# The ninth product of a tile's first quarter goes to SBUF and its transfer folds four planes

## What is computed

```python
x = x + _L0_conv_ref(_gn(x), ...)   # signs, 3x3 depthwise, prelu, bn, sign, 1x1, prelu, bn, + residual
x = x + _L1_conv_ref(_gn(x), L1_conv_W, L1_conv_b)

def _L1_conv_ref(x, W, b):          # K = 3
    filters = einsum('bchw,oc->bohw', x, W) + b            # 9 filters for each channel and pixel
    filters = filters.reshape(B, C, 9, H, Wd).transpose(0, 1, 3, 4, 2)
    patches = _extract_patches(x)                          # the 9 neighbours of each pixel
    return sum(patches * filters, axis=-1)
```

## Time and profile before

| what | us |
|---|---|
| median of three runs | 720.24 |
| the profiled execution | 720.51 |
| span of that execution | 718.6 |
| DVE busy | 657.9 |
| PE busy | 623.5 |
| POOL busy | 603.3 |
| ACT busy | 553.6 |
| DMA, queue of the folds (q0), share of 16 engines | 58.3% |
| DMA, queue of loads, stores and mirrors (q1), share | 27.8% |

### The profile page before, as it was taken

How to read it: one execution, slowest core, us unless ns; L and a number is a source line. 1 busy time by engine, 2 the same in 40 slices (tenths; PEclk the granted TensorE clock), 3 DMA queues, 4 the chain that set the end, 5 groups by cost and what they waited for, 6 DMA issues and landing times.

```text
span 718.6 us, 18827 instructions
## 1 busy us (share of the span) xinstructions
PE 623.5 (87%) x8017; PEld 254.4 (35%) x8017; DVE 657.9 (92%) x998; ACT 553.6 (77%) x822; POOL 603.3 (84%) x264
## 2 busy tenths in 40 slices
PE   2539889899998989899898989899999989899897
PEld 1224333333333334343333334333333334342333
DVE  3729879999999999999999999999999999999886
ACT  6885998897979788887978898897979888836110
POOL 2002658899999999989899999999999999999896
PEclk9859989999999999999999999999999999999899
DMA  5225767899999999998999999999999997998884
GB/s 202 87 58 148 131 153 196 190 251 207 227 226 196 233 203 245 205 252 187 230 219 182 244 204 250 206 246 215 223 229 193 240 202 162 203 191 176 193 172 136
DMA packets 34280, 142.11 MB, mean 198 GB/s; under 512 B 3348, under 2 KB 11540, under 8 KB 32276
## 3 DMA queue, kind: packets, MB, share of 16 engines
q0 software_dynamic: 17232, 75.87, 58.3%
q1 hardware_dynamic: 16940, 65.03, 27.8%
q10 hardware_dynamic: 24, 0.00, 0.0%
HBM read 26.03 MB, written 25.69 MB: 72 GB/s over the span
## 4 chain that ended last, share of the span: by engine, by line
POOL 48%; DVE 30%; ACT 7%; issue 6%; PE 4%; DMA 3%; SPq 1%; POOLq 0%; DVEq 0%; ACTq 0%
DVE prod L946 25%; POOL prod L386 17%; POOL ob L410 10%; POOL prod L399 10%; POOL prod L368 6%; POOL prod L377 3%; DVE xb L917 3%; PE tap_ps L478 3%; DMA mirror<-q 2%; ACT unused L581 2%; POOL prod L392 2%; ACT st L581 1%; ACT signs L581 1%; ACT ab L581 1%; DMA xb<-in_x_dram 1%
## 5 line engine op out<-in xcount | busy, mean ns | idle before, releaser
L478 PE MATMUL tap_ps<-q,w_t 64*64 64x392 f32 x2304 | 472.1, 506 | 52.1 <-DMA mirror<-q 20.5
L946 DVE SCALAR_TENSOR_TENSOR prod<-tap_ps,bias,q 128x784 f32<-128x784 f32 x493 | 487.4, 1026 | 31.4 <-PE tap_ps L478 26.0
L478 PE MATMUL tap_ps<-mirror,w_t 64*64 64x392 f32 x2304 | 467.4, 507 | 0.0
L478 PEld LDWEIGHTS tap_ps<-q,w_t 64*64 64x64 f32 x2304 | 151.2, 134 | 263.1 <-DVE prod L946 172.6
L386 POOL TENSOR_TENSOR prod<-prod 128x2352 f32<-128x2352 f32 x45 | 240.2, 5337 | 0.0
L368 POOL DMA_DIRECT2D prod<-prod x63 | 75.0, 1190 | 91.3 <-DVE prod L946 91.0
L521 PE MATMUL tap_ps<-signs,dw_diag 64*64 64x392 bf16 x2304 | 135.5, 342 | 9.8 <-DVE dw_diag L846 1.8
L478 PEld LDWEIGHTS tap_ps<-mirror,w_t 64*64 64x64 f32 x2304 | 139.4, 134 | 0.4 <-issue 0.4
L581 ACT ACTIVATE ab<-tap_ps,col 128x784 bf16<-128x784 f32 x128 | 120.5, 993 | 18.1 <-PE tap_ps L521 18.0
L410 POOL TENSOR_TENSOR ob<-prod 128x784 f32<-128x784 f32 x63 | 124.8, 1981 | 6.8 <-POOL prod L399 0.5
L581 ACT ACTIVATE st<-st 128x1 f32<-128x1 f32 x368 | 88.6, 252 | 36.5 <-DVE st L794 24.7
(11 more groups left out here) (117 smaller groups left out, 309.5 us busy)
## 6 DMA issues: line engine op xcount, KB each, us to landing
prod<-prod POOLq DMA_DIRECT2D x63, 1176.0 KB, 10.1
out_dram<-ob SPq DMA_DIRECT2D x31, 784.0 KB, 7.4
xb<-in_x_dram SPq DMA_DIRECT2D x15, 1568.0 KB, 15.7
mirror<-q SPq DMA_DIRECT2D x64, 203.0 KB, 4.3
xb<-in_x_dram SPq DMA_DIRECT2D x2, 784.0 KB, 5.8
out_dram<-ob SPq DMA_DIRECT2D x2, 392.0 KB, 2.3
prod<-in_L_conv_W_dram SPq DMA_DIRECT2D x1, 288.0 KB
prod<-in_L_conv_pw_weight_dram SPq DMA_DIRECT2D x1, 32.0 KB
```

Source lines behind the costliest of these rows:

```text
L478: mm = pe.matmul(rows3(tap_ps[to, slot, side, 0:CH]), w_t[own, k, :], moving, start=True, stop=True)
L946: v.scalar_tensor_tensor(place.rearrange("p j (a b) -> p j a b", b=WD), psum.rearrange("p j (a b) -> p j a b", b=WD), s_(t, B4) if k == 4 ...
```

## The change

In quarter 0 of all tiles but the last the ninth product now goes to SBUF like that of the other quarters (`POOLED` has 0 too), so that DVE's pair and POOL's early sum fall away there and ACT adds the mean to plane 8. Its fold (`fold_four`) waits for eight products and adds planes 0 to 3 onto planes 4 to 7. POOL's wide sum adds planes 6 and 7 onto 4 and 5, `add35` adds plane 8 onto 4, and the output sum takes planes 5 and 4. `PAIRED` is empty, so the branches of `in_pairs` make nothing. The delays of the steps on a quarter change, and with them most offsets in `COURSE`, `EARLY` and `PROLOGUE`, by 0 to 13 units.

```diff
+        def in_fours(g):
+            return on_pool(g) and g % QUARTERS in FOURS
...
+            def fold_four(t, qq):
+                g = quarter(t, qq)
+                wait(pool, prod_done, KK * g + 8)
+                pool.dma_start(prod[:, g % BUFS, 4:8, :], prod[:, g % BUFS, 0:4, :], accum_op=ALU.add,
+                               max_dma_last_dim=8 * QP).then_inc(folded[g % BUFS], 16)
...
                 pool.wait_ge(folded[g % BUFS], 16 * (g // BUFS + 1))
-                if on_pool(g):
+                if in_fours(g):
+                    pool.tensor_tensor(pr[:, 4:6, :], pr[:, 4:6, :], pr[:, 6:8, :], ALU.add).then_inc(summed_wide, 1)
+                elif on_pool(g) and not in_pairs(g):
                     pool.wait_ge(mean_added, with_mean(g))
...
-                if on_pool(g):
+                if in_fours(g):
+                    pool.wait_ge(summed_wide, g + 1)
+                    pool.wait_ge(mean_added, with_mean(g))
+                    pool.tensor_tensor(pr[4], pr[4], pr[8], ALU.add).then_inc(summed35, 1)
...
-                pool.tensor_tensor(ob[:, qq, :], pr[3], pr[4], ALU.add).then_inc(summed, 1)
+                pool.tensor_tensor(ob[:, qq, :], pr[5] if in_fours(g) else pr[3], pr[4], ALU.add).then_inc(summed, 1)
             for g in units:
-                for what, delay in ((fold, FOLD_DELAY), (add_early, EARLY_ADD_DELAY), (add_wide, WIDE_ADD_DELAY),
+                for t, qq in quarters(g, FOLD_DELAY):
+                    if not in_fours(quarter(t, qq)) and not (t.last and qq == QUARTERS - 1):
+                        fold(t, qq)
+                for t, qq in quarters(g, FOLD_FOUR_DELAY):
+                    if in_fours(quarter(t, qq)):
+                        fold_four(t, qq)
+                for what, delay in ((add_early, EARLY_ADD_DELAY), (add_wide, WIDE_ADD_DELAY),
                                     (add35, LATE_ADD_DELAY), (final, OUT_DELAY)):
...
 COURSE = {
-    'load': -106,
+    'load': -104,
...
-    'var1': -11,
-    'root1': -10,
-    'invert1': -10,
-    'q0': -8,
+    'var1': -12,
+    'root1': -11,
+    'invert1': -11,
+    'q0': -6,
     'q1': -4,
...
-AB_DELAY = 2
+AB_DELAY = 4
...
-FOLD_DELAY = 4
-EARLY_ADD_DELAY = 12
+FOLD_DELAY = 1
+EARLY_ADD_DELAY = 10
 MEAN_DELAY = 13
-WIDE_ADD_DELAY = 19
-LATE_ADD_DELAY = 25
-POOLED = 1, 2, 3
+WIDE_ADD_DELAY = 17
+LATE_ADD_DELAY = 20
+POOLED = 0, 1, 2, 3
+FOURS = 0,
+PAIRED = ()
+FOLD_FOUR_DELAY = 6
...
-TAKE_DELAY = 15
+TAKE_DELAY = 16
...
-OUT_DELAY = 27
+OUT_DELAY = 25
```

More of the change, by code:

```diff
@@ L199, in on_pool, with in_pairs, paired_early @@
             return g % QUARTERS in POOLED and g < (TILES - 1) * QUARTERS
+        def in_fours(g):
+            return on_pool(g) and g % QUARTERS in FOURS
+        def in_pairs(g):
+            return on_pool(g) and g % QUARTERS in PAIRED
+        def paired_early(g):
+            return sum(is_kept(n) or in_pairs(n) for n in range(g + 1))
         def in_banks(g):
@@ L373, in add_early @@
                 pr = planes(g)
+                if in_pairs(g):
+                    pool.wait_ge(prod_done, KK * g + 8)
+                    pool.tensor_tensor(pr[6], pr[6], pr[7], ALU.add).then_inc(summed67, 1)
                 if is_kept(g):
@@ L390, in add_wide @@
                     else:
-                        pool.wait_ge(summed67, kept(g))
+                        pool.wait_ge(summed67, paired_early(g))
                     pool.tensor_tensor(pr[:, 3:5, :], pr[:, 3:5, :], pr[:, 5:7, :], ALU.add).then_inc(summed_wide, 1)
@@ L396, in add35 @@
                 pr = planes(g)
-                if on_pool(g):
+                if in_fours(g):
+                    pool.wait_ge(summed_wide, g + 1)
+                    pool.wait_ge(mean_added, with_mean(g))
+                    pool.tensor_tensor(pr[4], pr[4], pr[8], ALU.add).then_inc(summed35, 1)
+                elif in_pairs(g):
+                    pool.wait_ge(summed_wide, g + 1)
+                    pool.wait_ge(mean_added, with_mean(g))
+                    pool.tensor_tensor(pr[3], pr[3], pr[8], ALU.add).then_inc(summed35, 1)
+                elif on_pool(g):
                     pool.wait_ge(summed_wide, g + 1)
@@ L1003 @@
 COURSE = {
-    'load': -106,
[L1005 to L1014, removed]
+    'load': -104,
+    'sum0': -71,
+    'mean0': -71,
+    'sign0': -67,
+    'square0': -63,
+    'var0': -61,
+    'root0': -55,
+    'invert0': -56,
+    'scales0': -54,
+    'inv_z': -52,
+    'ratio': -51,
     'job0': -56,
-    'job1': -43,
-    'job2': -32,
+    'job1': -44,
+    'job2': -37,
     'job3': -27,
-    'sum1': -20,
-    'mean1': -19,
-    'square1': -13,
-    'var1': -11,
-    'root1': -10,
-    'invert1': -10,
-    'q0': -8,
+    'sum1': -18,
+    'mean1': -17,
+    'square1': -11,
+    'var1': -12,
+    'root1': -11,
+    'invert1': -11,
+    'q0': -6,
     'q1': -4,
-    'b4': -1,
+    'b4': -2,
 }
@@ L1030 @@
     0: {
-        'sum0': -71,
-        'mean0': -105,
-        'sign0': -68,
+        'sum0': -72,
+        'mean0': -100,
+        'sign0': -69,
         'square0': -68,
[L1035 to L1038, removed]
+        'var0': -67,
+        'root0': -60,
+        'invert0': -66,
+        'scales0': -57,
         'inv_z': -60,
         'ratio': -60,
[L1041 to L1047, removed]
+        'job0': -66,
+        'job1': -65,
+        'job2': -60,
+        'job3': -59,
+        'sum1': -51,
+        'mean1': -47,
+        'square1': -49,
         'var1': -45,
@@ L1051 @@
         'q0': -44,
-        'q1': -43,
-        'b4': -40},
-    1: {
-        'sum0': -99,
-        'mean0': -98,
-        'sign0': -86,
+        'q1': -40,
+        'b4': -37},
+    1: {
+        'sum0': -102,
+        'mean0': -100,
+        'sign0': -88,
         'square0': -82,
         'var0': -82,
-        'root0': -82,
+        'root0': -83,
         'invert0': -80,
-        'scales0': -75,
-        'inv_z': -36,
+        'scales0': -77,
+        'inv_z': -37,
         'ratio': -36,
-        'job0': -39,
+        'job0': -38,
         'job1': -29,
@@ L1070 @@
         'mean1': -10,
-        'square1': -8,
+        'square1': -9,
         'var1': -9,
-        'root1': -8,
+        'root1': -9,
         'invert1': -8,
-        'q0': -8,
-        'q1': -8,
-        'b4': 0},
+        'q0': -9,
+        'q1': -5,
+        'b4': 1},
     2: {
         'sum0': -62,
[L1080 to L1090, removed]
+        'mean0': -65,
+        'sign0': -55,
+        'square0': -54,
+        'var0': -50,
+        'root0': -49,
+        'invert0': -48,
+        'scales0': -48,
+        'inv_z': -40,
+        'ratio': -35,
+        'job0': -40,
+        'job1': -34,
         'job2': -32,
@@ L1095 @@
 PROLOGUE = {
-    'bias': -52,
-    'turn_w': -41,
+    'bias': -59,
+    'turn_w': -44,
     'copy_w': -45,
[L1099 to L1103, removed]
+    'signs_rest': -38,
+    'square_0': -51,
+    'square_1': -60,
+    'square_2': -53,
+    'square_3': -46,
 }
-AB_DELAY = 2
+AB_DELAY = 4
 RELU_DELAY = 6
```

## The result

The changed kernel takes 710.0 us, the median of four runs (706.91 to 717.21), beside 720.29 for the kernel before on the same chip: a ratio of 0.9867, with a 95% interval of 0.983 to 0.9903. The forecast was 722.8. The profiled execution took 709.95 us, with a span of 708.0; before, 720.51 and 718.6.

The account below looks back on a forecast made before the run. The DMA was taken to bound the changed kernel's loaded tiles at 41.1 us: +6.4 for ten loaded tiles and -3.8 for four others added 2.6 to 720.51, giving 723.1, or 722.8 us as the median. The range was 703 to 730.

Parts of the forecast that it names:

- ten loaded tiles of 41.1 us: Sum: ten tiles that carry a load go from 40.46 to 41.1 us each, together +6.4 us.
- four others: Sum: four tiles with DMA to spare save 0.95 us each, together -3.8 us.
- the moved places at nothing: Moved step offsets: steady ones cost nothing, the earlier var1 shuffle gives back up to 0.95 us; start 0, 2 us either way.
- the list of laps: Per-tile bounds compared: DVE 38.6 us, POOL 39.15, the DVE-POOL loop some 38.1, and the DMA 41.1.
- DVE, POOL: Engine work per tile: DVE falls from 39.5 to 38.6 us, POOL's lap rises from 38.9 to 39.15.
- What bounds the kernel: Kernel before: DVE, POOL and DMA stand within 1 us of the tile's length; the wait chain alternates between POOL and DVE.
- the mixed one: Loop over DVE and POOL, output sum to output sum: 40.1 us before, some 38.1 after the change.
- ACT's work at nothing: 15 added mean additions of 0.94 us cost nothing, since ACT idles 2.19 us a tile ahead of `scaled`.
- the prediction's second case: Rival, chance 0.20: recorded DMA occupancy is stretched by 2 us a tile, so POOL's lap of 39.15 sets tiles: 703.4 us.
- The DMA at 41.1: Loaded tiles: 39.3 us of DMA work plus 1.8 for the fourth fold plane makes 41.1 us, the bound; chance 0.70.
- The late landing: Rival, chance 0.10: quarter 0's fold lands after 16.7 us, POOL waits 3.5 us a tile, lap 42.65, total 738 us.
- First tiles at nothing: Prologue and first tiles: moved places there priced at 0, with 2 us to either side.

Follow-up runs that it names:

- e6: Changed kernel with three-plane folds in quarter 0 too, POOL adding the other planes by an early sum and add35: 723.49 us.
- e1: Changed structure of quarter 0 with its delays, but COURSE, EARLY, PROLOGUE and AB_DELAY of the kernel before: 725.95 us.
- e11: e1 with ACT's added mean addition cut to 8 of 784 columns: 723.43 us.
- e12: e10 with sum1 and mean1 two units later and invert0 one unit earlier: 741.83 us.
- e14: e12 with AB_DELAY 4 instead of 2, so every conv on ACT comes two units later: 720.61 us.
- e5: Changed kernel with four-plane folds in all four quarters, not only quarter 0: 798.55 us in its one run.
- e13: Changed kernel with the matmuls that read q alone issued before the wait for the mirror, in each half's first unit: 707.84 us.
- e3: Changed kernel loading only the first quarter of each tile's pixels for tiles 3 to 15: 702.0 us.
- e8: e1 with the changed kernel's COURSE and AB_DELAY, keeping the old EARLY and PROLOGUE: 721.95 us.
- e9: e1 with the changed kernel's EARLY and PROLOGUE, keeping the old COURSE and AB_DELAY: 733.95 us.
- e10: e1 with six steps of the first normalisation, var0 to ratio, issued 1 to 7 units later: 729.53 us.
- e15: e14 with job1 one unit and job2 five units earlier: 748.74 us.
- e16: e1 with job1 one unit and job2 five units earlier: 763.43 us.

## Why the prediction was wrong, step by step

The forecast had a loss: ten loaded tiles of 41.1 us for +6.4, four others for -3.8. What came is -7.1 over twelve laps and -3.5 by tile 2. The step that gave the wrong sign is the DMA as the bound of the loaded tiles, at 41.1 us. A second term, the moved places at nothing, hides 16 us, most of which a loop that the list of laps lacked takes back.

**DVE, POOL.** Both laps were right. DVE is busy 38.69 us a tile after (38.6 computed), the changed kernel's lap is POOL's 39.15 and 0.7 of waits, and e6 has 40.88 for 40.96.

**What bounds the kernel.** For the kernel before this held: its chain runs over POOL and DVE, 48% and 30%, with ACT at 7%. For the changed kernel the list of laps (DVE, POOL, the mixed one, the DMA) lacked one, the loop over ACT, DVE, the mirror and PE. With the structure and the old offsets it is the longest, 41.03 us (e1). The prediction looked at its end only, the shuffle of var1. And it read the 2.19 us of ACT ahead of `scaled` as idle time that covers 0.94 of work. From before to e1 the stretch ahead of that wait grew by 0.81 us, and the wait shrank by 0.45 only, since ACT waits there for a result that its own earlier relu released.

**ACT's work at nothing.** The number held (e11: no change of the laps, 2.5 us of 726), for another reason than the one given: in e11 PE waits longer for the mirror by what ACT saves.

**The moved places at nothing, 2 us either way.** With the structure they are worth 16 us (e1 to after), 1.13 us of each lap and some 4 by tile 2; without them the change loses. The prediction looked at the queues of POOL and SP, which keep their order; the moves that matter are on ACT, DVE and PE. e12 and e14 show 0.8 of the 1.13: root0 and scales0 between the last relu and sum1, with the next tile's first conv behind them. In the sum this omission and that of the loop over ACT nearly cancel: with both left out and the DMA out of the way, the sum is the prediction's second case, 703.4, which has no waits of POOL and no gain at the start. That the forecast of 722.8 lies near e1's 725.95 is luck: 41.1 us of DMA is not what holds e1's tiles of 41.03, since e14 has the same transfers in laps of 40.23.

**The DMA at 41.1.** This is the step that failed in the sum. The share came as forecast, 1.00, and POOL does wait for folds, but by 0.34 us a tile, in laps of 39.90. A fourth plane at 1.8 us was fair: 2.1 of lap where the transfers set it (e5). Wrong was the sum's other part, 39.3 us of work in a tile of before, read from the share. e13 needs no more than its lap, 39.57, with the fourth plane in it; so before needed at most 37.5 (an estimate, 39.57 less e5's 2.1; with the prediction's lower end of 1.0 for a plane it would be 38.6). The prediction argued from two tiles with 4.42 us for each MB; e3 shows nearly the same folds at two different occupancies. In its second case, "the DMA gives way", 2 us of stretch were named; by that estimate it gave way by 1.8 (39.3 to 37.5). The Trainium skill's fit ("DMA: Bandwidth & Descriptors", "Anatomy of one DMA — SWDGE (gpsimd) path"), by which the prediction had 714, gave a nearer time, but by luck: it too takes the DMA as the bound, and its 0.92 us for the plane is not what e5 measured.

**The late landing.** It came in part: in the kernel after, POOL waits for a four-plane fold 3.3 us in five tiles from 190 to 640 us. Such a fold lands 13.1 us after its issue (the median), not 16.7. In e12, where it lands after 14.8, the wait is 1.7 us a tile.

**First tiles at nothing.** 3.5 us were won there by tile 2, outside the 2 us allowed. In e8 and e9, with one half of the offsets each, tile 2 comes later than in e1; by which step of the start isn't settled.

## What to carry to other kernels

When engines hand a tile's results around, list the closed loops that cross several engines, also those that the change could make the longest. Any loop's pieces add up to the lap; the bound is the loop without slack, where each step starts when the one before it in the loop ends, and the chain of waits shows which that is. Here the change shortened the loop that was the bound (POOL and DVE), and without the moved steps another (ACT, DVE, the mirror, PE) came out longer. A wait inside such a loop covers added work only in part, or not at all. Moving a step helped where it went to a place at which the loop itself waits, with nothing queued ahead of it that waits longer (e14, and not e10 or e12). Offsets of a hand-made order are a set: parts of a good set were slower than either whole one (e9, e12, e15, e16).

A DMA share of 98% isn't a bound by itself. Ask how the recorded occupancy moves when another queue's bytes go away.

## What was not expected of the hardware

A fold's recorded occupancy depends on its company: 52 MB of folds took 68.5% of 400 us beside 41 MB of other transfers and 73.2% beside 29 MB.

After a wait of 1.26 us of TensorE for the mirror stretches of 4 us have a granted clock of 0.81 and 0.76, and in another tile, after 1.49 us, of 0.57, between its two levels of 1.2 and 2.4 GHz; the tile became some 2.3 us longer. Not every wait does it: from 190 to 640 us there were eight waits for the mirror and two such tiles. The spread of the changed kernel's times fits: the run of 706.91 us has a mean granted clock of 0.979, that of 717.21 has 0.966. That the clock makes this whole difference isn't shown.
